# One decoder block on one core: a query projection moved into another slot, layer norm 2 split into two parts, and separate buffers in the last two routed tiles

## The reference

```
self attention : 16 heads of 64, softmax(q k^T / 8) v, then w_out and b_out
cross attention: 16 heads of 16, keys and values from ctx (375 per batch), mask, Wq Wk Wv Wo with biases
feed forward   : y = down[e] (silu(gate[e] x) * up[e] x) with e = argmax(router x)   (8 experts, hidden 512)
                 ys = the same with shared weights; x + y + ys
layernorm(x)   = (x - mean) / sqrt(var + 1e-5)
```

## Time and profile before

| | us |
|---|---|
| median of 3 runs | 419.44 (418.94 to 420.23) |
| the profiled execution's own time | 416.93 |
| span of its instructions | 415.2 |
| TensorE matmul busy | 394.6 (95%) |
| VectorE busy | 252.2 (61%) |
| ScalarE busy | 207.2 (50%) |
| GpSimd busy | 51.1 (12%) |
| TensorE clock granted, mean | 0.994 of full |

### The profile page before, as it was taken

One profiled execution on the slowest core, in us unless ns is written; L12 is line 12 of the kernel. 1 busy time (PEld: TensorE's weight loads), 2 busy tenths in 40 slices (PEclk: granted clock), 3 DMA queues, 4 the chain that ended last, 5 costly groups with the idle time before them and its releaser, 6 DMA issues.

```text
span 415.2 us, 12975 instructions
## 1 busy us (share of the span) xinstructions
PE 394.6 (95%) x5102; PEld 295.4 (71%) x5103; DVE 252.2 (61%) x729; ACT 207.2 (50%) x605; POOL 51.1 (12%) x80
## 2 busy tenths in 40 slices
PE   8989999999999999999999999999899999999991
PEld 7857877878787766666666666666565476899981
DVE  1376767856766877576768676868673642244443
ACT  1063444442716457777668566768683104345530
POOL 4010001101010101000010101010100054213333
PEclk9999999999999999999999999999999999999997
DMA  8997200000000014042222221910000013112210
GB/s 270 367 385 251 59 3 3 2 4 2 6 2 3 4 39 152 3 188 76 117 73 118 106 86 39 414 44 2 2 2 2 1 65 101 63 52 72 73 40 30
DMA packets 15255, 34.48 MB, mean 83 GB/s; under 512 B 2381, under 2 KB 9150, under 8 KB 13920
## 3 DMA queue, kind: packets, MB, share of 16 engines
q1 hardware_dynamic: 13952, 30.72, 21.0%
q0 software_dynamic: 1104, 2.76, 1.9%
q10 hardware_dynamic: 144, 0.23, 0.2%
HBM read 27.27 MB, written 6.70 MB: 82 GB/s over the span
## 4 chain that ended last, share of the span: by engine, by line
PE 45%; issue 38%; DVE 9%; ACT 4%; POOL 3%; DMA 1%; POOLq 0%; DVEq 0%; ACTq 0%
PE banks L458 11%; PE banks L846 6%; PE banks L480 4%; PE banks L917 4%; PE banks L927 3%; ACT p L998 3%; PE banks L938 3%; PE banks L858 3%; PE banks L500 3%; PE banks L522 3%; PE banks L535 3%; DVE p L1182 2%; DVE pT L1191 1%; DVE nm L1174 1%; POOL rstd L373 1%
## 5 line engine op out<-in xcount | busy, mean ns | idle before, releaser
L1317 DVE CUSTOM_DVE_ANT_0 p<-banks,mask 112x375 f32<-112x375 f32 x128 | 62.6, 542 | 24.0 <-PE banks L649 23.9
L1054 ACT ACTIVATE p<-p,nm 112x375 f32<-112x375 f32 x128 | 73.8, 603 | 5.3 <-DVE nm L1317 5.2
L1061 ACT ACTIVATE pT<-banks 128x336 f32<-128x336 f32 x96 | 42.4, 443 | 42.2 <-PE banks L669 41.9
L998 ACT ACTIVATE p<-banks,nm 128x112 f32<-128x112 f32 x128 | 43.4, 365 | 32.1 <-DVE nm L1174 32.1
L669 PEld LDWEIGHTS banks<-ident,p 112*128 112x128 f32 (+1 forms) x384 | 38.4, 140 | 28.9 <-issue 21.9
L669 PE MATMUL banks<-ident,p 112*128 112x112 f32 (+1 forms) x384 | 53.2, 266 | 1.9 <-DVE nm L1317 1.5
L458 PE MATMUL banks<-x2T,arena 128*128 128x224 f32 x256 | 51.6, 357 | 0.0
L458 PEld LDWEIGHTS banks<-x2T,arena 128*128 128x128 f32 x256 | 47.6, 190 | 1.7 <-issue 0.5
L373 POOL TENSOR_TENSOR rstd<-veps,minus_half 128x1 f32<-128x1 f32 x14 | 7.7, 551 | 278.1 <-DVE veps L1206 278.1
L1167 DVE TENSOR_SCALAR arena<-banks 128x448 f32<-128x448 f32 x32 | 19.6, 617 | 22.8 <-PE banks L458 22.8
L649 PE MATMUL banks<-kT,qz 32*112 32x375 f32 x256 | 28.8, 516 | 1.7 <-ACT pT L1061 0.8
(11 more groups left out here) (147 smaller groups left out, 591.3 us busy)
## 6 DMA issues: line engine op xcount, KB each, us to landing
arena<-in_ug SPq DMA_DIRECT2D x8, 1024.0 KB, 5.8
arena<-in_dn SPq DMA_DIRECT2D x8, 512.0 KB, 6.8
mid<-in_ctxT SPq DMA_DIRECT2D x8, 375.0 KB, 3.2
slots_s<-blank SPq DMA_DIRECT2D x14, 128.5 KB
arena<-in_wqk SPq DMA_DIRECT2D x7, 256.0 KB, 5.0
slots_x<-blank SPq DMA_DIRECT2D x14, 128.0 KB
p<-slots_s SPq DMA_DIRECT2D x9, 128.5 KB, 2.0
kT<-slots_x SPq DMA_DIRECT2D x9, 128.0 KB, 2.1
```

The lines of the kernel that those rows point to most:

```text
L998: e = act.activation(p1[g][:, i], PE_S1[g % 2][:, i * 128:i * 128 + S], ACT.Exp, bias=nm1[:, n:n + 1], accum_out=rs1[:, n:n + 1])
L1054: act.activation(p2[i % RING], p2[i % RING], ACT.Exp, bias=nm2[:, i % H:i % H + 1], scale=-1.0).then_inc(exp2, 1)
L1061: act.activation(pT2[:, i % RING], PE_T2[r][:, 0:KT * S].rearrange("p (k n) -> p k n", k=KT), ACT.Copy).then_inc(pt2_act, 1)
L1317: v.tensor_tensor_reduce(p2[i % RING], PE_S2[r][0:S, 0:S2], bias[:], 1.0, 3e38, ALU.add, ALU.min, accum_out=nm2[:, i % H:i % H + 1]).then_ ...
```

## The change

Four edits. (1) The query projection of batches 2 and 4 goes from place 2 of the second slot to place 0 of the third; the turn of the output, which stood there, goes to place 2 of the third slot in these two batches. VectorE's query drain goes from behind the second slot to ahead of the fourth row extreme of the third slot, where that of batch 0 already was. (2) Layer norm 2's moments follow its addition at once, ahead of the first slot's row extremes; its last part goes from the beginning of the second slot to the end of the first. (3) The product of the last routed tile is written to a part of `mid` that is free by then and no longer waits for the down product of the tile before. (4) The last tile but one uses buffer 1 and a scatter semaphore of its own, the last uses buffer 0 and waits for the scatter of the last but two. GpSimd's loop does one tile less, and that tile is written out behind it.

```diff
-            sp.wait_ge(stored, tiles * 16)
+            sp.wait_ge(stored, tiles * 16 - 16)
+            sp.wait_ge(stored_other, 16)
...
-            with g.Fori(0, tiles - 1) as t:
+            with g.Fori(0, tiles - 2) as t:
                 root3(t, 0)
                 to_out(t, 0)
-            root3(tiles - 1, 1)
-            to_out(tiles - 1, 1)
+            root3(tiles - 2, 1)
+            to_out(tiles - 2, 1, stored_other)
+            root3(tiles - 1, 0)
+            to_out(tiles - 1, 0)
...  TensorE, between(n, place)
-                if (g, place) == (1, 2) and b in (2, 4):
+                if (g, place) == (2, 0) and b in (2, 4):
                     pe.wait_ge(k_sb, (b + 2) * KC)
                     project_q(b // 2 + 1)
-                if (g, place) == (2, 0) and b >= 1:
+                if (g, place) == (2, 2 if b in (2, 4) else 0) and b >= 1:
                     if b in (2, 4):
                         pe.wait_ge(q_sb, b // 2 + 2)
...
-            down(tiles - 1, d, False)
+            down(tiles - 1, d, False, hrT_last)
...  VectorE, between(n, place)
                 if (g, place) == (0, 0) and b >= 3:
                     ln2_add(b - 3)
+                    ln2_a(b - 3)
...
                 if (g, place) == (0, 4) and b >= 3:
-                    ln2_a(b - 3)
+                    ln2_b(b - 3)
...
-                if (g, place) == (1, 0) and b >= 3:
-                    ln2_b(b - 3)
-                if (g, place) == (1, 4) and b in (2, 4):
+                if (g, place) == (2, 2) and b in (0, 2, 4):
                     evac_q(b // 2 + 1)
-                if (g, place) == (2, 2) and b == 0:
-                    evac_q(1)
...  VectorE, finish(t, first, p=0, kept=0)
                 if not first and p == 0:
-                    v.wait_ge(stored, t * 16)
+                    v.wait_ge(stored, t * 16 - kept)
...
-            product(tiles - 1, False)
-            finish(tiles - 2, False)
-            finish(tiles - 1, False, 1)
+            product(tiles - 1, True, hrT_last)
+            finish(tiles - 2, False, 1)
+            finish(tiles - 1, False, 0, 16)
```

More of the change, by code:

```diff
@@ L179, in build @@
         lgT = mid[:, 0, 0:2 * TILE]
-        hr = mid[:, 0, 0:HID]
+        hrT_last = mid[:, 0, 0:HID].rearrange("p (k n) -> p k n", k=HT)
         hrT = spent[:, 2 * C:2 * C + HID].rearrange("p (k n) -> p k n", k=HT)
@@ L234, in build @@
             sem(n) for n in ("xst_pe", "xst_sb", "gu_pe", "g_sb", "h_sb", "wg_sb", "wu_sb", "yr_pe"))
-        sum3, ids_sb, stats3, aggr3, ve3s, rstd3, done3, stored = (
-            sem(n) for n in ("sum3", "ids_sb", "stats3", "aggr3", "ve3s", "rstd3", "done3", "stored"))
+        sum3, ids_sb, stats3, aggr3, ve3s, rstd3, done3, stored, stored_other = (
+            sem(n) for n in ("sum3", "ids_sb", "stats3", "aggr3", "ve3s", "rstd3", "done3", "stored", "stored_other"))
         PE_S1, PE_J1, PE_U1, PE_W1 = bank[0:2], bank[2:4], bank[4:8], bank[7][:, 256:512]
@@ L422, in root3, with to_out @@
                 g.tensor_tensor(rs3[:, p:p + 1], ve3[:, p:p + 1], minus_half[:], ALU.pow).then_inc(rstd3, 1)
-            def to_out(t, p):
+            def to_out(t, p, done=stored):
                 g.wait_ge(done3, t + 1)
@@ L427, in to_out @@
                 g.indirect_dma_start(flat, bass.IndirectOffsetOnAxis(ids[:, p:p + 1], 0), fin[p], None,
-                                     bounds_check=T - 1, oob_is_err=False).then_inc(stored, 16)
-            with g.Fori(0, tiles - 1) as t:
+                                     bounds_check=T - 1, oob_is_err=False).then_inc(done, 16)
+            with g.Fori(0, tiles - 2) as t:
                 root3(t, 0)
                 to_out(t, 0)
-            root3(tiles - 1, 1)
-            to_out(tiles - 1, 1)
+            root3(tiles - 2, 1)
+            to_out(tiles - 2, 1, stored_other)
+            root3(tiles - 1, 0)
+            to_out(tiles - 1, 0)
         @block.tensor
@@ L929, in up, with down @@
                 mm.then_inc(gu_pe, 1)
-            def down(t, e, first):
+            def down(t, e, first, h=hrT):
                 pe.wait_ge(h_sb, t + 1)
@@ L937, in down @@
                 for m in range(HT):
-                    mm = pe.matmul(YB[:, 0:C], hrT[:, m, :], arena[:, bass.ds(e[m], C)], start=(m == 0), stop=(m == HT - 1))
+                    mm = pe.matmul(YB[:, 0:C], h[:, m, :], arena[:, bass.ds(e[m], C)], start=(m == 0), stop=(m == HT - 1))
                 mm.then_inc(yr_pe, 1)
@@ L1495, in evac_x, with product @@
                 v.tensor_copy(xsT, bank[0][:, 0:KC * 128].rearrange("p (k n) -> p k n", k=KC)).then_inc(xst_sb, 1)
-            def product(t, first):
+            def product(t, first, h=hrT):
                 v.wait_ge(g_sb, t + 1)
@@ L1501, in product, with finish @@
                     v.wait_ge(yr_pe, t)
-                v.tensor_tensor(hrT.rearrange("p k n -> p (k n)"), gr[:], bank[4][:], ALU.mult).then_inc(h_sb, 1)
-            def finish(t, first, p=0):
+                v.tensor_tensor(h.rearrange("p k n -> p (k n)"), gr[:], bank[4][:], ALU.mult).then_inc(h_sb, 1)
+            def finish(t, first, p=0, kept=0):
                 v.wait_ge(yr_pe, t + 1)
```

## The result

| | before | changed |
|---|---|---|
| median of 6 runs each, us | 419.8 (418.94 to 425.85) | 415.03 (414.02 to 416.72) |
| ratio, 95% interval | | 0.9895 (0.987 to 0.992) |
| profiled execution: own time / span | 416.93 / 415.2 | 415.26 / 413.5 |
| cross stage, first to last score | 154.29 | 150.50 |
| last product of the loop (L1502) to last scatter | 12.50 | 11.81 |

One run of the kernel before, 425.85, lies over 1.5% above its fastest and is left out of the ratio. The forecast was 414.8, from 413.4 to 416.7. A second measurement of the same two kernels, on another occasion, gave 0.9893 (0.9863 to 0.9923).

The account below looks back on a forecast made before the run. TensorE's work plus a few waits bounds the cross stage; a chain through VectorE, GpSimd and two transfers sets the end. Gains of 3.81 + 0.8 = 4.6 us from 419.44 gave 414.8 us, range 413.4 to 416.7.

Parts of the forecast that it names:

- Layer norm 2: Cross stage, second slots: row extremes no longer 0.81 us late; 0.35 less each in batches 3 to 6, 0.81 in batch 7.
- The covers it named: First slots: 1.34 us of idle VectorE before the first row extreme covers the moved chain, 0.41 to spare, cost 0.
- Rival (a): Second slots: ScalarE takes VectorE's place, so batches 3 to 6 give nothing there; price 1.4 us, 416.2; chance 0.10.
- The query projection: Batches 2 and 4: second slots lose 2.00 and 2.71 us, third slots gain 1.38 each; net 0.62 and 1.33.
- Batch 0 was the right model: Third slots of batches 2 and 4: batch 0, with projection and drain already there, gives their new length, 5.94 us.
- Rival (b): Third slots of batches 2 and 4: work and wait add in full, +2.34 instead of +1.38 each; 416.7; chance 0.08.
- The sum of the stage: Cross stage: gains of batches 2 to 7 from layer norm 2 and the query projection, together 3.81 us.
- The end: Last routed tiles: product runs beside the down product, sum 0.60 us earlier; 0.8 taken in all, 0.6 to 0.85.
- The token numbers: Last tile but one: without the wait for the scatter before, they follow the sum, 0.78 us earlier.
- Rival (c): End: something between GpSimd's last two scatters sets it, 0.8 less, 415.6; counterargument: late token numbers set their distance; chance 0.05.
- Rival (d): First slots: moments delay row extremes; beyond 0.41 us each microsecond costs five; uncovered 6.8 us, 421.6; chance 0.03.
- The 0.56 for the keys: Batch 4, second slot: projection's wait for ScalarE's copy of the keys, counted within the query projection's 2.71 us loss.

Follow-up runs that it names:

- the home alone: Only the last product's own place in `mid`, on the kernel before, with buffers and scatter waits unchanged; end 12.50 us, one execution.
- the buffers alone: Only the two buffers swapped and the second scatter semaphore, on the kernel before; the product keeps its place and wait; end 12.30 us, one execution.
- the end alone: Only the edits of the last two routed tiles, on the kernel before; 417.86 us against 418.19, ratio 0.9984.
- the port: Kernel before with one more GpSimd wait: its bias addition comes after layer norm 2's last part (L1355); 416.77 us against 419.07, one execution.

## Why the prediction was right

- Layer norm 2 (0.35 in each of batches 3, 5, 6; 0.81 in batch 7): measured 0.35, 0.33, 0.34, 0.82. The covers it named held: 0.35 us of idle VectorE was left ahead of the first slot's row extremes. Rival (a), ScalarE in VectorE's place, is out. (The prediction speaks of six VectorE operations that move; four do, the three of the moments and the last part. Nothing is worked out from the six.)
- The query projection (0.62 in batch 2, 1.33 in batch 4): 0.60 and 1.31. Batch 0 was the right model, 5.94 for the third slot. Rival (b) is out.
- The sum of the stage was 3.81, measured 3.79 to 3.87 in two traces.
- The end: 0.8 worked out, 0.69 measured. Counted from the loop's last product, the sum moved from 5.90 to 5.42, so 0.48 and not 0.60. The down product ended at 401.42 + 1.89 = 403.31 and the sum came 0.23 behind it; the prediction put it where the product had started before, 0.11 behind the down product. This is the term that was off. What stands behind the sum moved with it: the last down product, which now ends the last wait. The token numbers moved 0.74 where 0.78 was worked out. Rival (c) is out, though not by the argument given: the two last scatters are as far apart as before, 2.97 and 2.98 us, and both came earlier.
- Rival (d) was rightly held unlikely, but priced wrongly: each microsecond beyond the slack does not cost five. Four of the five slots have a key projection on TensorE that covers another 0.5 us. With the chain lengthened by four operations (1.41 us) the stage grew by 2.8 us; by the prediction's price, five times 1.41 - 0.41, it would have been 5.
- The attribution in batch 4 was incomplete. The 0.56 for the keys was booked to the query projection's move; the layer norm's move alone takes it away as well. And the row extremes of this slot were 1.20 late, not 0.81: the 0.35 ahead of the aggregate was not seen. The total is right all the same, because the whole slot was priced by that of a sibling without any of this, and not by its parts.
- The prediction took the profiled execution of before, 2.5 us under the median, as a fair base for differences. It was, for the stage and the end. It would have misled in the comparison of two traces' spans: 1.7 us there, 4.8 in the medians. The last 0.2 us between 414.8 and 415.03 say nothing: the median of the kernel before moved by 0.4 between the two sets of runs.

**What lies in the middle.** From the last score to the last product of the loop, fourteen traces gave 93.3 to 96.3 us. From the last score to the first load of gathered rows it is 39.41 to 39.56 in all of them, 39.55 before and 39.54 after: the stage's gain is carried that far whole. Two delays behind that load make the rest. The first is at the first tile: VectorE's copy of the turned tile comes 2.8 to 3.0 us after the load's issue in nine traces and 5.4 to 5.6 in five, and the second tile's turn is then 1 us later. The second is at the third tile, whose turn stands for its load. In the changed kernel's first trace, which has both (TensorE and SyncE's queue):

```profile
359.18 4.48 SPq L314 DMA_DIRECT2D kT<-slots_x  x2
...
362.69 0.44 PE L910 MATMUL banks<-ident,kT 128*128 128x128 f32 x2 [1.52 <-DMA kT<-slots_x]
```

The turn came 3.5 us after the load's issue; in the kernel before 361.69 to 363.67, 2.0. Against the kernel before, the second delay cost 1.53 and the first 1.33, together the difference of 2.84 within some hundredths. The changed kernel's second trace has neither in this size, and 94.02. The first delay shows with the old cross stage as well (the home alone, the buffers alone), and so does the second (the end alone, the port). So they belong to the execution and not to the change; what makes them is open.

## What to carry to other kernels

Compare equal steps of a periodic stage by the distance between their starts, in the same trace: a sibling step that already has the new order gives its price to a few hundredths. Look for the covered slack on both sides of an added chain, on the engine itself and on the one that waits for it, before pricing its failure. When two waits end close together, price them together: here one edit alone gave nothing, the other 0.20 us, and both 0.69. And before moving work out of a late chain, look whether something makes it slow where it stands: one wait on GpSimd gave 1.85 us of the 3.13 that the moved layer norm gave.

## What was not expected of the hardware

- An SBUF-to-SBUF scaling on VectorE (128x256, float32) took 404 to 414 ns alone and 0.81 us when GpSimd's addition of the same size (0.73 us) had started 0.07 us before it; the mask operation, with one operand in PSUM, took 533 to 551 ns in all 128 instances of the kernel before and of the changed one, those beside the addition included.
- The same load of 128 rows right behind scatters let the turn that needs it go 2.0 to 3.5 us after its issue, from one execution to the next, and the first score of the cross stage came between 151.3 and 154.1 us; the cross stage itself repeated within 0.2 us in the four traces that have it as before (154.20 to 154.39).
